# A memset ahead of each indirect DMA on GpSimd, and the second image's row stores in one run

## What is computed

```python
x = _L0_conv_ref(x, ...)                       # group norm, attention, projection, + input
t = _to_tokens(x)
t = t + _L1_attn_ref(_ln_t(t), ...)            # linear attention
# _L1_ffn_ref, on _ln_t(t):
logits = xt @ Wr + br
top_p, top_idx = jax.lax.top_k(softmax(logits), 2)
weights = top_p / top_p.sum(axis=-1, keepdims=True)
h = gelu(einsum('end,edh->enh', xe, W1) + b1)  # xe: layer norm of the token, by expert
y = einsum('enh,ehd->end', h, W2) + b2
out = (weights * y of the two experts taken).sum()
t = t + out
```

## Time and profile before

| | us |
|---|---|
| median of 3 runs | 384.41 (383.03 to 385.42) |
| the profiled execution | 384.25 |
| its span, first to last instruction | 382.5 |
| TensorE busy | 333.5 (87%) |
| VectorE busy | 202.0 (53%) |
| ScalarE busy | 204.1 (53%) |
| GpSimd busy | 110.7 (29%) |
| mean granted TensorE clock, full is 1 | 0.94 |

### The profile page before, as it was taken

One profiled execution on the slowest core, in us unless ns is written; L12 is line 12 of the kernel. 1 busy time (PEld: TensorE's weight loads), 2 busy tenths in 40 slices (PEclk: granted clock), 3 DMA queues, 4 the chain that ended last, 5 costly groups with the idle time before them and its releaser, 6 DMA issues.

```text
span 382.5 us, 6582 instructions
## 1 busy us (share of the span) xinstructions
PE 333.5 (87%) x2004; PEld 211.0 (55%) x2004; DVE 202.0 (53%) x616; ACT 204.1 (53%) x324; POOL 110.7 (29%) x140
## 2 busy tenths in 40 slices
PE   7979799899999989999998496987573889999996
PEld 3533343343333335345532354976472879999996
DVE  2584444563756553655576247468521255777620
ACT  1460765666577554645585023648341467777732
POOL 2182391000000001000306730042565644444430
PEclk9985989999999999999999879798799699999999
DMA  6078768660000025000001102001121222222415
GB/s 187 2 153 192 173 144 340 150 252 25 0 2 3 3 62 160 0 2 1 2 0 43 50 15 63 17 14 37 49 62 50 69 66 71 70 71 75 143 39 209
DMA packets 21772, 29.28 MB, mean 77 GB/s; under 512 B 4055, under 2 KB 15628, under 8 KB 21484
## 3 DMA queue, kind: packets, MB, share of 16 engines
q1 hardware_dynamic: 16808, 18.04, 17.7%
q0 software_dynamic: 3744, 10.31, 8.5%
q10 hardware_dynamic: 1188, 0.53, 0.6%
HBM read 11.62 MB, written 9.25 MB: 55 GB/s over the span
## 4 chain that ended last, share of the span: by engine, by line
PE 71%; DVE 16%; issue 5%; another core or an unknown queue 3%; ACT 2%; DMA 1%; DVEq 0%; POOL 0%; SPq 0%; POOLq 0%
PE ps L865 13%; PE ps L1082 12%; PE ps L1069 11%; PE ps L827 6%; PE ps L846 5%; DVE above L1190 4%; PE ps L707 2%; PE ps L807 2%; PE ps L923 2%; PE ps L747 2%; PE ps L900 2%; PE ps L779 2%; PE ps L892 1%; DMA Qs<-mrow 1%
## 5 line engine op out<-in xcount | busy, mean ns | idle before, releaser
L559 ACT ACTIVATE probs<-ps 128x1024 f32<-128x1024 f32 x64 | 65.3, 1021 | 37.0 <-PE ps L846 36.9
L865 PE MATMUL ps<-probs,vT 128*32 128x512 f32 x256 | 68.3, 609 | 1.1 <-ACT probs L559 1.1
L1082 PE MATMUL ps<-w,GT 128*128 x368 | 54.0, 293 | 17.1 <-ACT GT L685 14.0
L865 PE MATMUL ps<-probs,ones 128*32 128x512 f32 x256 | 68.4, 609 | 0.0
L1190 DVE CUSTOM_DVE_ANT_0 above<-ps,above 128x512 f32<-128x512 f32 x56 | 38.7, 691 | 40.8 <-PE ps L827 39.0
L1082 PEld LDWEIGHTS ps<-w,GT 128*128 128x128 f32 x368 | 48.5, 206 | 19.5 <-issue 19.2
L497 POOL DMA_INDIRECT token_out<-Y,yidx x46 | 44.0, 957 | 46.9 <-DVE Y L1481 44.4
L433 POOL TENSOR_TENSOR rstd<-ve,minus_half 128x1 f32<-128x1 f32 (+2 forms) x6 | 10.3, 1723 | 161.9 <-DVE ve L1232 88.6
L1069 PE MATMUL ps<-XTT,w1s 128*128 128x128 f32 x368 | 52.7, 290 | 4.8 <-issue 4.8
L685 ACT ACTIVATE GT<-H 128x512 f32<-128x512 f32 x46 | 28.9, 629 | 43.9 <-DVE H L1470 31.5
L1069 PEld LDWEIGHTS ps<-XTT,w1s 128*128 128x128 f32 x368 | 48.6, 205 | 6.0 <-issue 6.0
(11 more groups left out here) (196 smaller groups left out, 428.7 us busy)
## 6 DMA issues: line engine op xcount, KB each, us to landing
expert_in<-zeros POOLq DMA_DIRECT2D x2, 1495.0 KB, 7.7
XR<-expert_in SPq DMA_DIRECT2D x46, 65.0 KB
Qs<-q_hi SPq DMA_DIRECT2D x16, 128.0 KB, 2.8
w<-in_L_ffn_W SPq DMA_DIRECT2D x1, 2048.0 KB, 8.3
w<-in_L_ffn_W SPq DMA_DIRECT2D x8, 256.0 KB, 4.4
YG<-token_out SPq DMA_DIRECT2D x8, 256.0 KB, 4.1
Ks<-k_hi SPq DMA_DIRECT2D x14, 128.0 KB, 2.7
X<-in_x SPq DMA_DIRECT2D x2, 512.0 KB, 4.7
```

What stands on the lines that cost most here:

```text
L559: nc.scalar.activation(probs[:, s % 3, :], bank(2 + 2 * (s % 2), 2), ACT.Exp).then_inc(exp_done, 1)
L865: last = nc.tensor.matmul(bank(6 + o % 2)[i * HD:(i + 1) * HD, :], w, probs[:, s % 3, hd * HALF:(hd + 1) * HALF], start=kt == 0, stop=kt = ...
L1082: last = nc.tensor.matmul(bank(4 + p)[:, 0:D], GT[:, p, c, :], w2[:, e, c, :], start=c == 0, stop=c == HC - 1)
```

## The change

GpSimd gets a buffer `pause_at` of 128 x 64 float32 that nothing reads. Ahead of each of the 32 indirect stores and each of the 46 indirect sends it writes this buffer with a memset and waits for that write (`link`). In `send` the memset stands ahead of the wait for `y_sb`. In the first image's scatter `rsqrt(B + 2)` stands ahead of the stores of j = 6, so behind 12 stores instead of 14. The second image's 16 stores stand in one run, behind the sends of tiles 0 to 3; the sends of tiles 4 to 45 come all behind them.

```diff
@@ -35,6 +35,7 @@
     FILLERS = 6
     NBY = 16
     SENT_FIRST = 4
+    PAUSE = 64
     RW = D + 2
     EPS = 1e-5
     GROUPS = J // 2
@@ -99,6 +100,7 @@
         xn = sb("xn", [P, B, L])
         zeros, _ = at("zeros", [P, TILES, RW], f32, room[0])
         t2 = sb("t2", [P, B, J, P])
+        pause_at = sb("pause_at", [P, PAUSE])
         X2 = sb("X2", [P, B, J, RW])
         kd = [at(f"kd{b}", [P, HALF], f32, room[0] - 4 * HALF * (b + 1))[0] for b in range(B)]
         Kd, o = at("Kd", [P, B, HEADS0, HALF], f32r, w2_at)
@@ -482,17 +484,18 @@
                 link(nc.gpsimd.iota(X2[:, b, :, D], [[2, J]], base=2 * b * L, channel_multiplier=2 * J,
                                     allow_small_or_imprecise_dtypes=True))
 
-            def scatter(b, between, behind=lambda j: None):
+            def scatter(b, between):
                 pool.wait_ge(slots_ready, b + 1)
                 pool.wait_ge(x2_ready, b + 1)
                 for j in range(J):
                     between(j)
                     for w in range(2):
+                        link(nc.gpsimd.memset(pause_at[:, :], 0.0))
                         pool.indirect_dma_start(xs[:, :], bass.IndirectOffsetOnAxis(ap=slots[:, b, w, j:j + 1], axis=0),
                                                 X2[:, b, j, :], None).then_inc(scattered[b], 16)
-                    behind(j)
 
             def send(t):
+                link(nc.gpsimd.memset(pause_at[:, :], 0.0))
                 pool.wait_ge(y_sb, t + 1)
                 pool.indirect_dma_start(yt[:, :], bass.IndirectOffsetOnAxis(ap=yidx[:, t:t + 1], axis=0),
                                         Y[:, t % NBY, :], None).then_inc(y_sent[t % NBY], 16)
@@ -500,12 +503,12 @@
             rsqrt(B)
             rsqrt(B + 1)
 
-            scatter(0, lambda j: rsqrt(B + 2) if j == J - 1 else None)
+            scatter(0, lambda j: rsqrt(B + 2) if j == J - 2 else None)
             rsqrt(B + 3)
             for t in range(SENT_FIRST):
                 send(t)
-            scatter(1, lambda j: None, lambda j: send(SENT_FIRST + j))
-            for t in range(SENT_FIRST + J, NT):
+            scatter(1, lambda j: None)
+            for t in range(SENT_FIRST, NT):
                 send(t)
 
         @block.scalar
```

## The result

| | before | changed |
|---|---|---|
| median of the runs timed together | 384.62 us | 379.56 us (379.32 to 381.56) |
| ratio to before (of the means, as all ratios here) | 1 | 0.9885, 95% interval 0.9839 to 0.9931 |
| span of the profiled execution | 382.5 us | 377.8 us |
| image 1's rsqrt on GpSimd starts | 225.44 | 218.66 |
| first run of stores, end of the last | 229.68 | 226.01 |

The change is worth 5 us by the medians (4.4 by the means) where 16.4 were forecast. The table holds the whole account: 7.7 us are won ahead of tile 5, 3.1 are lost between tiles 5 and 15, and 4.2 to 4.7 are left at the last send and at the end. Lines of the changed kernel are named by its own numbers, which stand 2 or 3 higher: L1484 is the addition of an expert result (L1481 before), L1085 and L1072 its matmuls, L494 and L500 the store and the send, L493 and L498 their memsets, L435 the rsqrt.

The account below looks back on a forecast made before the run. TensorE's late signals under dense indirect DMAs bound tiles 5 to 15; regaining 16.8 and 2 us, with GpSimd ending 2.4 later than TensorE, took 16.4 off the span: 366.1, about 368 us, range 362 to 388.

Parts of the forecast that it names:

- The late signals, and their cause: Both scatters: TensorE's completion signals come several us late during dense GpSimd indirect DMAs; 16.8 us lost between 275 and 311.
- The price of a DMA: Each GpSimd indirect DMA with its memset and wait takes 1.50 us, against 1.27; 1.42 from below, 1.75 for the range.
- While ... 1.27 us apart: Signals are late while indirect DMAs stand 1.27 us apart for over some 5 us, not at 1.9; 16.8 us regained.
- The first run of stores: First image's scatter: signal no longer late, rsqrt ends 5.2 us earlier; valued at 2 us, bounds -0.5 and 3.2.
- the forecast cost: TensorE idles longer ahead of the second image's projections, after which its granted clock falls; costs 1 to 3 us.
- GpSimd as the bound: Expert stage: 58 DMAs in one run at 1.50 us end the last send at 353.5, 2.4 later than by TensorE.
- frees nothing: Rival: GpSimd being busy at all may hold signals back, so the pause frees nothing; some +7.6, 392 us; chance 0.24.
- half is freed: Rival: half of the lost 16.8 us stays, or GpSimd's chain is longer than summed; 380 us; chance 0.20.

Follow-up runs that it names:

- c1: Changed kernel with image 1's sixteen indirect stores replaced by direct DMAs of the same rows into a region aside; 379.46 us, one execution.
- c2: Changed kernel with image 1's sixteen indirect stores replaced by GpSimd memsets of 960 columns, no DMA; 376.80 us, one execution.
- b1: Changed kernel with memsets of 320 columns from image 1's stores on, none ahead of the last 8 sends; 369.81 us, ratio 0.9617.
- b2: Changed kernel with memsets of 400 columns from image 1's stores on, none ahead of the last 8 sends; 372.49 us, ratio 0.9704.
- e1: Changed kernel without its 78 memsets, so the new order alone; 388.28 us, ratio to before 1.0030.
- e2: Kernel before with the memset ahead of each indirect DMA and nothing moved; 386.36 us, ratio 0.9963.
- e5: Changed kernel with memsets of 512 columns from image 1's stores and the sends of tile 4 on; 386.49 us, ratio 1.0000.
- a0_same_again: The changed kernel run once more, word for word; 383.1 us, ratio to before 0.9854.

## Why the prediction was wrong

**The late signals, and their cause: right.** Both runs of stores lose time because TensorE's completion signals come late while GpSimd issues indirect DMAs in a dense run. c1, c2, b1 and b2 show it, and that direct DMAs are harmless, as the early runs of them had suggested.

**The price of a DMA: too high, at the lower bound.** 1.50 was taken, 1.41 measured, the lower bound was 1.42. A DMA behind a memset takes 0.96 and not 1.06 (1.03 to 1.09 stand only where GpSimd had waited or computed), and where 0.30 stood between two DMAs there are now the memset's 0.17 and a wait of 0.28.

**"While ... 1.27 us apart": the step that failed.** I had rows at 1.27 (late) and at 1.9 (not late), and put 1.41 to 1.50 on the side of 1.9 without any row between. Measured, ten tiles take 38 to 40 us at 1.41, 22 to 27 at 1.57, 20.8 at 1.62, 19.4 at 1.69. The change stays on the wrong side: instead of -16.8 the term is +3.1, with results up to 11.8 us late. Why it is a loss, and not nothing, is open. Sixteen stores and five sends now follow one another without a wait for a Y, where before a send waited 1.96 us in between the earlier trace rows, and at 1.27 that order alone takes 38.7 us (e1) where the old one takes 35.9. But at 1.41 the old order takes 40.1 (e2), no less than the new.

**The first run of stores: right in kind, too small.** L1210 was forecast for 211 to 212 and starts at 210.08; the rsqrt was to end at 221.9 and ends at 220.3. But I valued it at 2 us, with 3.2 as the most, and it brought 7.7 in this profile and 3.0 in the repeat. Two deductions were wrong. The last store ends at 226.01, not 227.9, so the two tile copies end at 230.65 (229.84 + 0.81) instead of 233.1, and the key exponential starts 6.0 earlier than before. And the clock took nothing back in this profile: TensorE idles longer ahead of the second image's projections, as forecast (1.43 us ahead of L926, before not at all), but the clock is 1.00 from 217 to 227 us. It falls later, to 0.85 and 0.81 between 227 and 237 us, behind 2.44 us of idling, and is back at 1.00 from 237 to 246 us, where before it was 0.62. There L941 takes 2.05 us (3.06 before) and a group of L1072 1.06 (1.92), which is about the rest of the 7.7. In the repeat the forecast cost did come: 3.35 us idle ahead of L926, and its sixteen matmuls took 5.41 us instead of 3.72.

**GpSimd as the bound: didn't come about.** With TensorE held, the sends caught up at 293 us. The step itself was sound: where the signals are on time (b2, e5) the tiles are done 10 and 18 us before the last send starts. That it starts at 354.5 in b2, where the forecast had it end at 353.5, is chance: the DMAs there are 1.69 apart and not 1.50, the last eight sends have no pause, and the run begins 5.5 us earlier than forecast.

**The rival "frees nothing"** had its condition right (a run at this space holds signals like one at 1.27) for the second run and wrong for the first. Its 5.7 us of loss measure 3.1, and the first run turned its sign. The outcome, 379.6, lies where "half is freed" had put it (380), by another way: not half of one stall, but part of the first of two. That it lies there is luck.

**Still open.** What in an indirect DMA holds the signals; that it is not its bytes, rows, or GpSimd's busy time is shown. Whether the signal itself is late or the end of the matmul's writing: the profile models the ends of matmuls, and all it shows is that TensorE starts its next group while the result before is not yet taken. And what decides, at 1.41 us, whether a signal of the first run is hit: the profiles with that space in the first run have the rsqrt anywhere from 218.4 to 222.8, and two of the same program differ by 2.3.

## What to carry to other kernels

Where a threshold lies between two measured states and a change lands between them, one doesn't know on which side; the forecast has to carry both as near equals, or the change has to go well across. Pace a resource by the chain that it disturbs and by its own total: here 1.62 us a DMA gives 0.962 of the time, 1.69 gives 0.970, 1.41 gives 0.985 to 0.989 and 1.78 gives 1.00, since at the one end signals are late and at the other 58 DMAs are themselves the end. And where a wait ends long after its matmul and the releaser has no name, look at what GpSimd issues just then.

## What the hardware showed that I had not expected

- A finished result of TensorE is taken up to 16.3 us late (a0_same_again) while indirect DMAs go out 1.41 us apart. To ten tiles' 19 us, 1.57 us apart still adds 3 to 8, and 1.69 nothing; sixteen direct DMAs 1.45 apart of the same bytes leave it on time.
- The lateness did not go away with fewer bytes (8 or 520 a row) or rows (64 or 128) of the DMA.
- Signals between the other engines are on time in the same run: ScalarE starts on the H of 284.10 at 284.83, 0.04 us behind its end.
- A dense run costs twice: TensorE, idle in between, has a granted clock of 0.75 for 34 us (1.00 in b2), so the work between two late signals is slower too.
- Memsets on GpSimd of 64, 320, 400 and 960 columns took 0.17, 0.38, 0.45 and 0.90 us. The narrowest, put between two indirect DMAs, adds only 1.41 - 1.27 = 0.14 us: the 0.28 of its wait takes the place of the 0.30 that stood there anyway, and its own 0.17 comes on top.
